# A third buffer for the streamed w1 tiles in the expert stage, with the b2 load moved to the end

## The reference

```python
h = jax.nn.gelu(jnp.einsum('bsd,edh->bseh', x, w1) + b1, approximate=False)
expert_out = jnp.einsum('bseh,ehd->bsed', h, w2) + b2
sel = jnp.take_along_axis(expert_out, top_i[..., None], axis=2)
return (top_p[..., None] * sel).sum(axis=2)
...
x = _layernorm(x + _L0_ffn_ref(x, ...), axis=-1)
```

## Time and profile before

| | us |
|---|---|
| median of 3 runs | 6016.24 |
| the three runs | 6316.73, 5792.43, 6016.24 |
| profiled execution | 5799.52 |
| its span, slowest core (core 2) | 5797.8 |
| spans of the 8 cores | 5777.5 to 5797.8 |
| TensorE busy | 4666.2 (80%) |
| ScalarE busy | 932.8 (16%) |
| VectorE busy | 1004.0 (17%) |
| GpSimd busy | 326.0 (6%) |

### The profile page before, as it was taken

How to read it: one execution, slowest core, us unless ns; L and a number is a source line. 1 busy time by engine, 2 the same in 40 slices (tenths; PEclk the granted TensorE clock), 3 DMA queues, 4 the chain that set the end, 5 groups by cost and what they waited for, 6 DMA issues and landing times.

```text
span 5797.8 us, 73994 instructions; the slowest of 8 cores (5777.5 to 5797.8 us)
## 1 busy us (share of the span) xinstructions
PE 4666.2 (80%) x30120; PEld 3018.3 (52%) x30120; DVE 1004.0 (17%) x3101; ACT 932.8 (16%) x1493; POOL 326.0 (6%) x622
## 2 busy tenths in 40 slices
PE   8866655566379899898989889898988989898993
PEld 8433333333137465564746556473756647374662
DVE  1355544554201000000100000010100001010004
ACT  0011111111120211112020211203021120302112
POOL 1000000000010100001010000001000000101000
PEclk5865556555599999999999999999999999999996
DMA  6210000000343343434334343434334343433431
GB/s 158 52 25 15 19 19 19 19 14 15 94 93 69 55 77 56 76 62 69 70 59 73 59 72 60 73 59 73 70 60 72 62 70 62 71 68 57 77 61 58
DMA packets 121851, 346.71 MB, mean 60 GB/s; under 512 B 32874, under 2 KB 33002, under 8 KB 112370
## 3 DMA queue, kind: packets, MB, share of 16 engines
q0 software_dynamic: 86768, 281.11, 29.0%
q1 hardware_dynamic: 34754, 60.87, 3.3%
HBM read 601.97 MB, written 20.97 MB: 107 GB/s over the span
## 4 chain that ended last, share of the span: by engine, by line
PE 68%; DMA 15%; DVE 7%; issue 6%; ACT 3%; another core or an unknown queue 1%; DVEq 0%; ACTq 0%; POOLq 0%; SPq 0%; POOL 0%
PE pb L1013 31%; PE pb L987 22%; DMA w1b<-w 14%; PE pb L571 2%; PE pb L256 2%; PE pb L737 2%; PE pb L625 1%; PE pb L452 1%; PE pb L476 1%; ACT hT L995 1%; PE pb L810 1%; PE pb L316 1%; PE pb L664 1%; DVE comb L583 1%
## 5 line engine op out<-in xcount | busy, mean ns | idle before, releaser
L987 PE MATMUL pb<-x1T_sb,w1b 128*128 128x512 bf16 x8192 | 1865.1, 384 | 480.1 <-DMA w1b<-w 335.2
L1013 PE MATMUL pb<-w2b,hT 128*128 128x256 bf16 x16384 | 1791.1, 273 | 16.7 <-ACT hT L995 16.7
L1013 PEld LDWEIGHTS pb<-w2b,hT 128*128 128x128 bf16 x16384 | 1602.0, 98 | 209.3 <-issue 24.2
L987 PEld LDWEIGHTS pb<-x1T_sb,w1b 128*128 128x128 bf16 x8192 | 779.9, 98 | 1561.9 <-issue 718.0
L995 ACT ACTIVATE hT<-pb,b1all 128x512 bf16<-128x512 f32 x1024 | 703.5, 687 | 3261.6 <-PE pb L987 3261.6
L1023 DVE SCALAR_TENSOR_TENSOR acc<-pb,c_sb,acc 128x256 f32<-128x256 f32 x512 | 247.5, 483 | 3905.7 <-PE pb L1013 3905.7
L94 POOL DMA_DIRECT2D w1b<-w x512 | 270.2, 528 | 2065.1 <-PE pb L987 2032.9
L638 ACT ACTIVATE Pt<-pb 128x512 bf16<-128x512 f32 x256 | 149.4, 597 | 387.1 <-PE pb L625 387.1
L625 PE MATMUL pb<-QT,Kroll 128*128 128x128 bf16 x1024 | 144.9, 302 | 31.2 <-PE pb L664 7.9
L664 PE MATMUL pb<-Vroll,Pt 128*128 128x65 bf16 x1024 | 98.3, 237 | 66.0 <-DVE Pt L644 39.4
L790 PE MATMUL pb<-id_f,x_tc 128*128 128x128 f32 x128 | 34.8, 427 | 130.3 <-DVE x_tc L779 104.6
(11 more groups left out here) (127 smaller groups left out, 1466.7 us busy)
## 6 DMA issues: line engine op xcount, KB each, us to landing
w1b<-w POOLq DMA_DIRECT2D x512, 256.0 KB, 3.8
w2b<-w POOLq DMA_DIRECT2D x64, 2048.0 KB, 14.4
x_in<-x_comb SPq DMA_DIRECT2D x34, 512.0 KB, 3.9
x_tc<-x_comb SPq DMA_DIRECT2D x16, 512.0 KB, 4.8
x1s<-x_tc SPq DMA_DIRECT2D x16, 512.0 KB, 2.6
acc<-x1s SPq DMA_DIRECT2D x1, 8192.0 KB, 57.9
out<-acc SPq DMA_DIRECT2D x16, 512.0 KB, 2.6
x1Ts<-x1T_tc SPq DMA_DIRECT2D x16, 256.0 KB, 2.8
```

Of the source, the lines that this page charges most:

```text
L987: e.matmul(PB[bk][:, :], w1b[sl][:, kc * 128:(kc + 1) * 128], x1T_sb[:, kc * 2048 + Tt * 1024 + nh * 512: kc * 2048 + Tt * 1024 + (nh + 1) ...
L1013: e.matmul(PB[ob][:, 0:256], hT[:, f * 1024 + tcl * 128: f * 1024 + tcl * 128 + 128], w2b[sl2][:, f * 256:(f + 1) * 256], start=(f == 0), ...
```

## The change

The w1b tiles get a third buffer. The first three loads are issued at the start, the load for step idx + 3 behind step idx, and three semaphores serve them. The tiles w1b, w2b and b1all are allocated in a scope of their own, which is closed after the last round; b2_sb is allocated behind it in the space that they leave. Its load, so far the first of GpSimd's loads in the stage, is now issued after the last round: it waits for the last matmul of phase 2, the last accumulation and the last Gelu.

```diff
--- before.py
+++ after.py
@@ -921,10 +921,12 @@
                 acc = sbf("acc", [128, NT * 1024], F32)
                 x1T_sb = sbf("x1T_sb", [128, 8 * 2048], BF16)
                 hT = sbf("hT", [128, 32 * 1024], BF16)
-                w1b = [sbf(f"w1b{i}", [128, 1024], BF16) for i in range(2)]
-                w2b = [sbf(f"w2b{i}", [128, 8192], BF16) for i in range(2)]
-                b1all = sbf("b1all", [128, 256], F32)
-                b2_sb = sbf("b2_sb", [8, 1024], BF16)
+                es_f1 = ExitStack()
+                def sbf1(name, shape, dt):
+                    return es_f1.enter_context(nc.sbuf_tensor(name, shape, dt))
+                w1b = [sbf1(f"w1b{i}", [128, 1024], BF16) for i in range(3)]
+                w2b = [sbf1(f"w2b{i}", [128, 8192], BF16) for i in range(2)]
+                b1all = sbf1("b1all", [128, 256], F32)
 
                 p.new_sem("accsem")
                 ACCL = p.dma("y", acc[:, :].rearrange("p (t c) -> p t c", t=NT),
@@ -932,16 +934,15 @@
                 p.new_sem("xtsem")
                 XTL = p.dma("y", x1T_sb[:, :].rearrange("p (k m) -> p k m", k=8),
                             x1Ts.rearrange("k p m -> p k m"), "xtsem", deps=FGATE)
-                p.new_sem("b2sem")
-                B2L = p.dma("g", b2_sb[:, :], b2_in, "b2sem", deps=FGATE)
                 p.new_sem("b1sem")
                 B1L = p.dma("y", b1all[:, :].rearrange("p (e f) -> p e f", e=8),
                             b1_in.rearrange("e p f -> p e f"), "b1sem", deps=FGATE)
+                for i in range(3):
+                    p.new_sem(f"w1sem{i}")
                 for i in range(2):
-                    p.new_sem(f"w1sem{i}")
                     p.new_sem(f"w2sem{i}")
 
-                w1_war = [None, None]
+                w1_war = [None, None, None]
                 w2_war = [None, None]
                 w1_tok = {}
                 w2_tok = {}
@@ -951,9 +952,9 @@
 
                 def load_w1(idx):
                     e_, Tt, f = seq_w1[idx]
-                    sl = idx % 2
+                    sl = idx % 3
                     tok = p.dma("g", w1b[sl][:, :], w1_in[e_, f, :, :], f"w1sem{sl}",
-                                deps=[w1_war[sl]] + (FGATE if idx < 2 else []))
+                                deps=[w1_war[sl]] + (FGATE if idx < 3 else []))
                     w1_tok[idx] = (tok, sl)
 
                 def load_w2(idx):
@@ -965,6 +966,7 @@
 
                 load_w1(0)
                 load_w1(1)
+                load_w1(2)
                 load_w2(0)
                 load_w2(1)
 
@@ -1000,8 +1002,8 @@
                                 h_rd[bk] = GL
                                 HDONE = GL
                             w1_war[sl] = tkmm
-                            if iw1 + 2 < len(seq_w1):
-                                load_w1(iw1 + 2)
+                            if iw1 + 3 < len(seq_w1):
+                                load_w1(iw1 + 3)
                             iw1 += 1
                         for dq in range(4):
                             tokw2, sl2 = w2_tok[iw2]
@@ -1034,6 +1036,11 @@
                         MM2LAST = tk2
 
                 ACCDONE = max(o_ev[0], o_ev[1], key=lambda t: t[1])
+                es_f1.close()
+                b2_sb = sbf("b2_sb", [8, 1024], BF16)
+                p.new_sem("b2sem")
+                B2L = p.dma("g", b2_sb[:, :], b2_in, "b2sem",
+                            deps=[MM2LAST, ACCDONE, h_rd[0], h_rd[1], h_rd[2], h_rd[3]])
 
                 p.new_sem("osem0")
                 p.new_sem("osem1")
```

## The result

The fastest executions of both kernels compared, the changed kernel takes 0.9351 of the time before (95% interval 0.9324 to 0.9378), 6.5% less; the profiled execution took 5422.22 us against 5799.52. The median over ten runs is 5897.74 us (5415.82 to 6140.58) against 6049.98 (5792.43 to 6318.23). These medians are higher than the profiled times because in many executions of either kernel the cores of one die ran at a lower granted clock than the others and ended later; the ratio leaves such executions out.

What follows compares the result with a forecast made beforehand. TensorE's two expert matmuls bound the kernel, the first idling for w1b loads that two buffers don't cover. 5799.5 us less 373 (351 from 15 phases, 22.5 from the first), plus 1 and 5, gave 5432; range 5390 to 5650.

Steps and rivals of the forecast that it cites:

- The sum: Whole execution: 5799.5 us less 373 for phases 1, plus 1 at stage start and 5 at the end: 5432 us.
- The pauses inside phases go: Phase 1: two steps, 6.90 us, cover a load's 4.6, ending pauses of some 1.1 us every second step; 0.5 kept.
- At a phase start the pause shrinks by one step and stays: Start of 15 later phases 1: stall behind the w2b load shrinks by 3.45, from about 9.1 to 5.7 us.
- The clock still falls, 2.0 us each: Behind each phase-start stall: slow clock still costs 2.0 us a phase, bounded by 0 and 2.0.
- Rival 4: Phase starts: the clock doesn't fall in the shorter stall, 30 us less, 5402; chance 0.07.
- The reason given: Phase-start stall: mean clock 0.63 over 9.65 us means some 2.5 us at full, then half; 5.7 is past that.
- b2 at the end: After the last round: nothing hides b2's load, so the bias add starts 5.2 us later; bounds 4.4 and 10.0.
- The third load at the start: Stage start: another 0.26 MB of w1b shares the DMA engines with x1T_sb; loss between 0 and 1.0 us, 1.0 taken.
- Rival 2: Phase 1 loads: 3.8 us is a rate, not a latency, so 162 us more than forecast, 5594; chance 0.05.
- Rival 3: Ahead of L987: the 66.9 us in 73 Gelu waits are real and stay, 5499; chance 0.04.
- Rival 1: TensorE in the stage: denser matmuls lower the clock; at 0.81, 818 us more, some 6250; chance 0.07, milder loss 0.03.
- the scaling: Range: the shown runs' median, 3.7% above the profiled execution, applied to the sum gives 5635, which the range holds.

Runs made afterwards that it cites:

- the half load: The kernel before, loading only the first half of each w1b tile after the first two tiles: 5581.0 us, a load landing after 2.9 us instead of 3.8.
- the kernel with longer steps and two buffers: The kernel before with four idle matmuls more in each step of phase 1, 4.32 us a step instead of 3.45: lowest time 6019.31 us, 6015.76 in a later run.

## Why the prediction was right in its working and wrong in its range

*The sum.* It gave 5432 us for an execution like the profiled one; that took 5422.22. Between the two traces the 15 later phases 1 give back 361.5 us (255.53 less 231.43, forecast 351), the first one 23.9 (forecast 22.5); the start costs 4.1 (forecast 1.0) and the end 4.1 (forecast 5.2). That accounts for the whole difference of the spans, 5797.8 to 5420.7. Point by point:

- The pauses inside phases go: right, none is left, and the 0.5 us a phase kept for late ones was not needed.
- At a phase start the pause shrinks by one step and stays: right. Forecast 5.7 us on average; the timeline shows 3.6 to 8.2, 5.4 on average, and the blocks of phase 2 are 231.4 us apart where 232 was forecast. The prediction let the load behind w2b land as it did before, after 10.9 to 12.7 us; it lands after 9.7 to 14.3, so the spread of the pauses was not foreseen and only their average was.
- The clock still falls, 2.0 us each: right. The 29 steps behind the pause take 101.7 to 103.2 us, where 100.3 is full clock by the 96.85 us for 28 steps with four buffers: 1.4 to 2.9 us, 2.1 on average, and 1.4 behind the shortest pause. Rival 4 is out. The reason given, some 2.5 us at full clock in the stall before the fall, does not carry over: in the pause of 3.6 us the clock stays at 1.00 and falls in the matmuls behind it.
- b2 at the end: forecast 5.2 us, measured as follows.

```profile
5314.17 0.48 DVE L1025 SCALAR_TENSOR_TENSOR acc<-pb,c_sb,acc 128x256 f32<-128x256 f32 x1 [3.01 <-PE pb L1015]
5315.45 0.52 POOL L94 DMA_DIRECT2D b_sb<-b  x1 [56.21 <-DVE acc L1025]
...
5317.70 1.01 PE L1052 MATMUL pb<-b_sb,cT 8*128 8x512 bf16 x2 [3.64 <-DMA b_sb<-b]
5318.95 0.69 DVE L1059 TENSOR_TENSOR acc<-acc,pb 128x512 f32<-128x512 f32 x1 [4.30 <-PE pb L1052]
```

From the end of the accumulation (5314.65) to the add are 4.30 us, 4.1 more than before. The landing was mis-sized, 2.1 us where w1b's 3.8 had been taken; the issue comes 0.8 us after its releaser instead of 0.5, and the two matmuls take longer, 1.01 us instead of 0.6.

- The third load at the start: forecast 1.0 us; the wait for x1T_sb went from 70.8 to 72.9 us, and in other kernels here it was between 69 and 76, so this isn't told from chance. The other 2.0 of the 4.1 us lie ahead of the stage, and the two traces are of different cores.
- Rival 2 (a rate) falls with the half load and with the changed kernel's own unbroken phases. Rival 3 (Gelu) falls with the waits: the changed kernel's L989 has none put down to the Gelu any more, so the 66.9 us of the earlier trace rows were w1b's.
- Rival 1 (the clock is lost to a denser stream): not in the profiled execution, where phase 2 and the body of phase 1 have 1.00. The limit of 13/16 that the Trainium skill tells of in "TensorE: Matmul & The Clock Gate", section "Seeing it yourself", is not seen there, though all eight cores run dense matmuls. (The rival's term is slightly off: 1/0.81 is 23.5% more, so 835 us where 818 stands.) But another trace here has the page's figure. It is one of the kernel with longer steps and two buffers that took 6566.62 us (stretch, length, busy by engine, then PEclk, DMA share, GB/s):

```profile
4200.00:4300.00 100.00, 99.85 (x728) 78.82 (x726) 10.64 (x22) 2.06 (x3) 2.11 (x4) 0.81 0.31 62
```

So rival 1's clock does occur with this kind of stream. No trace shows whether any execution of the changed kernel ran so.

*The range.* 5390 to 5650 was meant to hold the median of runs too, and that is 5897.74. The step that failed is the scaling: "Scaled by the same 3.7% it would be 5635". It took the distance of three runs' median from the profiled execution as a property of the kernel that a change keeps. It isn't: over ten runs it is 6049.98/5799.52, 4.3%, before and 5897.74/5422.22, 8.8%, after. Nor does one kernel keep it: in three more series of the kernel before the median lay 2.5% (7 executions), 4.4% (13) and 0.1% (7) above the lowest. Over so wide a spread a median falls wherever the middle execution happens to lie, between 5416 and 6141. Even the 4.3% of the ten runs before would have put the forecast at 5667, outside the range. The high end should have reached at least as far above the sum as the shown runs did above theirs (6316.73/5799.52, 8.9%: 5916).

Whether the change itself widens the distance isn't shown. The kernel with the third buffer alone, whose phases are the changed kernel's, had its median of six executions 2.5% above its lowest (5550.48 and 5417.64), so 8.8% need not be the change's.

## What to carry to other kernels

Compare the cycle of a buffer (wait, issue, landing, start) with the work that lies over it: n buffers give n - 1 steps of cover. With two buffers what was missing appeared as a pause every second step, even where the waits table puts it down to another engine. For a small load that stands in a queue behind a large one, a buffer more takes off one step of the wait and not the cause; cutting the large load into parts between the small ones takes the whole wait away, and cost nothing here. Where a time is to be forecast as a median of runs, take the spread of the runs shown as it stands, and not a factor from it.

## What the hardware showed that was not expected

- The first w1b load behind the 2 MB w2b load landed between 9.7 and 14.3 us after its issue in the changed kernel; in the kernel before it took 12.7 at the first phase start and 10.9 at the last. Why it varies more was not tried. The chain of waits of the changed kernel names the load one step later instead at some starts (12.19 us from 1850.39 at the first), so the issue has to be looked up.
- The granted clock can fall after a pause that has ended: 1.00 over a pause of 3.6 us, 0.58 over the 4 us of matmuls behind it. With two buffers and the load in parts, a pause of 3.2 us is followed by two steps of 8.75 us in place of 7.07.
- One execution of the two-buffer kernel with longer steps took 14122.67 us, 1.9 times the next longest (7454.38), with no cause that these runs show.
